# First stage of a fused decoder: four rounds as one program for each of two lanes, a new order of turns, and the extremes found a round later

## The reference

```
x = layernorm(x + L0_attn(x, W_f, b_f, W_i, b_i, W_h, b_h))   # gated linear recurrence along the sequence
x = layernorm(x + L0_xattn(x, ctx, Wq, Wkv, Wout, bout))      # 16 heads of 8, 256 queries, 64 context tokens
# the next block (L0_ffn) first needs max(abs(x)) over the WHOLE x, for its quantisation scale
```

## Time and profile before

| | |
|---|---|
| median of 3 runs | 3333.57 us (3331.22 to 3334.71) |
| the profiled execution | 3336.23 us, span 3334.4 us |
| first stage, from the first R1 on PE to the last norm | 21.9 to 352.2 us |
| busy over the whole span | PE 78%, PEld 56%, DVE 51%, ACT 30%, POOL 11% |
| mean granted TensorE clock | 0.911 of full |

### The profile page before, as it was taken

The page is one execution under the profiler, slowest core; times in us unless marked ns, Lnnn a source line. Parts: engine busy times, 40 slices in busy tenths (PEclk is TensorE's granted clock), DMA queues, the critical chain, the costliest instruction groups (busy, mean ns, idle before and its releaser), DMA issues.

```text
span 3334.4 us, 52950 instructions
## 1 busy us (share of the span) xinstructions
PE 2614.9 (78%) x23038; PEld 1875.8 (56%) x23038; DVE 1698.1 (51%) x4037; ACT 994.8 (30%) x1385; POOL 354.2 (11%) x605
## 2 busy tenths in 40 slices
PE   4666468888889887786687779877798777987778
PEld 3444146767777776654565555655556555565554
DVE  5555735565665654701367541675416654166541
ACT  3333312222322221021232432324323243232432
POOL 0111100110011100063111000110001100010000
PEclk8788658999999998986898999989999899998999
DMA  2000000000000000223600000000000000000000
GB/s 82 1 1 1 2 1 1 8 8 8 1 8 8 8 7 5 91 38 65 171 1 1 1 7 1 1 1 1 7 1 1 1 1 7 0 1 1 1 1 26
DMA packets 39354, 48.14 MB, mean 14 GB/s; under 512 B 7169, under 2 KB 36369, under 8 KB 38354
## 3 DMA queue, kind: packets, MB, share of 16 engines
q1 hardware_dynamic: 33490, 40.43, 4.1%
q0 software_dynamic: 5632, 4.33, 1.0%
HBM read 31.81 MB, written 12.91 MB: 13 GB/s over the span
## 4 chain that ended last, share of the span: by engine, by line
PE 56%; DVE 29%; ACT 6%; issue 4%; POOL 3%; DMA 1%; SPq 0%; DVEq 0%; POOLq 0%; ACTq 0%
PE banks L2396 7%; PE banks L870 6%; DVE wide_area L2272 4%; PE banks L2595 4%; DVE wide_area L1750 2%; PE banks L2385 2%; PE banks L1370 2%; PE banks L2170 2%; PE banks L1335 2%; PE banks L1169 2%; DVE xs L899 2%; DVE weights L2089 1%; PE banks L1403 1%; PE banks L1677 1%; PE banks L2179 1%
## 5 line engine op out<-in xcount | busy, mean ns | idle before, releaser
L2595 PE MATMUL banks<-wA 128*128 128x128 f32 x2664 | 366.9, 291 | 4.2 <-ACT gates L931 2.1
L2595 PEld LDWEIGHTS banks<-wA 128*128 128x128 f32 x2664 | 340.4, 205 | 23.2 <-issue 15.9
L891 DVE BATCH_NORM_STATS2 stats<-banks 128x6 f32<-128x128 f32 x208 | 46.4, 286 | 391.7 <-PE banks L870 363.8
L2272 DVE TENSOR_REDUCE wide_area<-banks 128x8 f32<-128x2048 f32 x64 | 146.8, 2293 | 103.4 <-PE banks L2170 103.4
L906 POOL TENSOR_TENSOR rstd<-moments,eps 128x4 f32<-128x4 f32 x56 | 11.2, 199 | 1431.7 <-DVE moments L895 1431.7
L2253 ACT ACTIVATE weights<-banks 128x2048 f32<-128x2048 f32 x64 | 120.1, 1877 | 96.1 <-PE banks L2179 96.1
L1750 DVE TENSOR_REDUCE wide_area<-banks 128x16 f32<-128x1024 f32 x80 | 94.1, 1218 | 53.2 <-PE banks L1663 53.1
L2396 PE MATMUL banks<-wide_area,big 128*128 128x512 f32 x192 | 85.7, 592 | 0.0
L899 DVE TENSOR_SCALAR xs<-banks,moments,rstd 128x128 f32<-128x128 f32 x208 | 70.9, 404 | 27.0 <-POOL rstd L908 25.5
L2089 DVE TENSOR_TENSOR weights<-banks,wC 128x2048 f32<-128x2048 f32 x32 | 72.2, 2287 | 24.0 <-PE banks L1976 24.0
L891 DVE BATCH_NORM_STATS2 dilvals<-banks 128x6 f32<-128x128 f32 x144 | 32.0, 285 | 96.8 <-PE banks L870 96.8
(11 more groups left out here) (761 smaller groups left out, 6124.8 us busy)
## 6 DMA issues: line engine op xcount, KB each, us to landing
big<-in_wE SPq DMA_DIRECT2D x1, 4096.0 KB, 12.6
weights<-long_kernel SPq DMA_DIRECT2D x8, 512.0 KB, 7.4
conv<-wide_area SPq DMA_DIRECT2D x16, 256.0 KB, 2.5
wC<-in_wC SPq DMA_DIRECT2D x1, 3012.0 KB, 16.7
wC<-in_wG SPq DMA_DIRECT2D x1, 2971.0 KB, 19.2
big<-in_wT SPq DMA_DIRECT2D x1, 2560.0 KB, 11.8
x_all<-in_xT SPq DMA_DIRECT2D x1, 2048.0 KB, 10.4
total<-spread SPq DMA_DIRECT2D x8, 256.0 KB, 2.2
```

The costliest lines, as they stand in the source:

```text
L891: dve.bn_stats(m.stats[:, i, :], self.tokens(i)).then_inc(*sg.up("dve", f"stats{i}"))
L2272: return dve.tensor_reduce(m.peaks[:, k % 2, :, :].rearrange("p t (r c) -> p r t c", r=4)[:, :, :, SPARE[j]], m.bank[:, :, :].rearrange("p ...
L2595: pe.matmul(bank[:, 0:P], m.ident, m.ident, start=True, stop=True)
```

## The change

The four rounds of a lane become one generator for each engine (`start_pe` and so on), and `turns` takes the steps of the two in the order of a string `FIRST` ("n" is lane 0, "f" lane 1), over all rounds at once. The three empty steps of lane 1 are gone. A lane's extremes of round it - 1 are taken in its own next R1, behind its minima, and after the last round only those of round 3 are left. `quant.dve` stands at the end of lane 1's round 0. "first norm" has 5 fillers, not 6.

```
-BUSY = {..., 'first norm': 6, ...}
+BUSY = {..., 'first norm': 5}
+FIRST = "nnffnnfnffnfnfnnfnffnfnfnfnfnfnfnfnfnfnffnnfnffnnnfnnffnfnffnfnfnfnfnfnfnfnfnfnnffnfnnfnfnffnfnnffnfnfnfnfnfnnfnfnffnfnfnfnfnfnfnfnnfnffnfnfnfnfnfnfnfnfnfnfnnfffnnf"
-        extreme = Signals(ctx, nc, "extreme", dve=each(ITERS, "high", "low"))
+        extreme = [Signals(ctx, nc, f"extreme{i}", dve="high low") for i in range(2)]
 first_pool:
-            yield from idle(LaneRecurrent.TICKS + i * LAG)
+            yield from idle(LaneRecurrent.TICKS)
 first_pe, first_act, first_dve:
-            yield from idle(i * LAG)
 first_dve:
-            yield from g.recurrent.dve(dve, it)
+            steps = g.recurrent.dve(dve, it)
+            next(steps)
+            if it:
+                extremes(dve, i, it - 1)
+            yield
+            yield from steps
+        def extremes(dve, i, it):
+            x, at = m.x_all[:, (2 * it + i) * T:(2 * it + i + 1) * T], 2 * it + i
+            dve.wait_ge(*first[i].norm[1].sig.done("act", "out", it))
+            dve.tensor_reduce(highest[:, at:at + 1], x, AX, ALU.max).then_inc(*extreme[i].up("dve", "high"))
+            dve.tensor_reduce(lowest[:, at:at + 1], x, AX, ALU.min).then_inc(*extreme[i].up("dve", "low"))
+        def start_dve(dve, i):
+            for it in range(ITERS // 2):
+                yield from first_dve(dve, i, it)
+                if it == 0 and i == 1:
+                    dve.wait_ge(loaded["wC"], 16)
+                    quant.dve(dve)
 on pool, pe and act, and likewise on dve:
-            for it in range(ITERS // 2):
-                weave(first_pe(pe, 0, it), first_pe(pe, 1, it), first_ticks, 0)
+            turns(start_pe(pe, 0), start_pe(pe, 1), FIRST)
 dve:
-            for it in range(ITERS // 2):
-                weave(first_dve(dve, 0, it), first_dve(dve, 1, it), first_ticks, 0)
-                if it == 0:
-                    dve.wait_ge(loaded["wC"], 16)
-                    quant.dve(dve)
-                else:
-                    extremes(it - 1)
-            extremes(ITERS // 2 - 1)
+            turns(start_dve(dve, 0), start_dve(dve, 1), FIRST)
+            for i in range(2):
+                extremes(dve, i, ITERS // 2 - 1)
```

More of the change, by code:

```diff
@@ L813 @@
 MIDDLE = "nfnfnfnfnfnfnfnfnfnffnfnfnnfnnfnnnffffnfnffnffnn"
-BUSY = {'first1': 2, 'dil_sum0': 7, 'wide scores1': 8, 'lead norm': 10, 'near norm': 1, 'dil_peaks1': 12, 'dil_peaks0': 2, 'lead product': 5, 'wide start': 2, 'gate': 7, 'back0': 3, 'first3': 1, 'first0': 1, 'first norm': 6, 'last norm 0': 9, 'last norm 1': 12, 'last norm 2': 9, 'last norm 3': 12, 'last norm 4': 12, 'last norm 5': 8, 'last norm 7': 1, 'last norm 8': 8, 'retention turned': 7, 'quant whole': 2, 'taken': 20, 'chosen': 5, 'choice start': 8, 'choice same': 4, 'choice bit': 3, 'choice rank': 24}
+BUSY = {'first1': 2, 'dil_sum0': 7, 'wide scores1': 8, 'lead norm': 10, 'near norm': 1, 'dil_peaks1': 12, 'dil_peaks0': 2, 'lead product': 5, 'wide start': 2, 'gate': 7, 'back0': 3, 'first3': 1, 'first0': 1, 'last norm 0': 9, 'last norm 1': 12, 'last norm 2': 9, 'last norm 3': 12, 'last norm 4': 12, 'last norm 5': 8, 'last norm 7': 1, 'last norm 8': 8, 'retention turned': 7, 'quant whole': 2, 'taken': 20, 'chosen': 5, 'choice start': 8, 'choice same': 4, 'choice bit': 3, 'choice rank': 24, 'first norm': 5}
 LAST = "nnfnnfnfnfnfnfnfnfnfnfnfnfnfnffnnnfnffnfnfnfnfnfnfnfnfnfnfnfnnfnfnffnfnfnfnfnfnfnfnfnfnfnfnfnnfnfnffnfnnffnfnfnfnfnfnfnfnfnfnfnfnfnfnfnfnfnfnfnfnfnfnfnfnfnfnfnfnfnfnfnfnfnfnfnfnfnfnfnfnffnfnfnfnffnffnnfnnff"
+FIRST = "nnffnnfnffnfnfnnfnffnfnfnfnfnfnfnfnfnfnffnnfnffnnnfnnffnfnffnfnfnfnfnfnfnfnfnfnfnnffnfnnfnfnffnfnnffnfnfnfnfnfnnfnfnffnfnfnfnfnfnfnfnfnnfnffnfnfnfnfnfnfnfnfnfnfnnfffnnf"
 MIDDLE_ALONE = "nnnnf" * 6
@@ L3243, in _ @@
             long_kernel.act(act)
-            for it in range(ITERS // 2):
-                weave(first_act(act, 0, it), first_act(act, 1, it), first_ticks, 0)
+            turns(start_act(act, 0), start_act(act, 1), FIRST)
             quant.act(act)
@@ L3296, in _ @@
             dve.tensor_scalar(bv2[:, 1:2], col["l1_bv"], 1.75, None, ALU.mult).then_inc(*const.up("dve", "bv_mid"))
-            dve.wait_ge(*extreme.done("dve", f"low{ITERS - 1}", 0))
+            for i in range(2):
+                dve.wait_ge(*extreme[i].done("dve", "low", ITERS // 2 - 1))
             xscale.dve(dve, (highest, lowest))
```

15 lines of the change are left out of this document (11 added, 4 removed).

## The result

The changed kernel took 3314.88 us (median of 10 runs, 3299.81 to 3333.83), the kernel before 3334.54 us (10 runs, 3329.93 to 3344.18): a ratio of 0.995, 95% interval 0.9933 to 0.9967. That is 19.7 us less, where 27 were forecast (3307); it lies in the range given.

The account below looks back on a forecast made before the run. The first stage was taken as bound by chains of waits between engines, no engine full. Order gains of 36.5 plus 0.6 at the end make 37, less 10 for the clock is 27: 3333.6 to 3307 us, range 3296 to 3327.

Parts of the forecast that it names:

- 10 for the clock: First stage: about two falls of PE's clock a round in the new period, 2.5 us lost a round, 10 in all.
- T: Start of the first lane's z in a round, from which the forecast counts its times; 19.62 us after round 2's first matmul.
- X6(0): Lane 0's step ending the first sequence: 29.4 us after T in round 1's order, 28.25 in rounds 0 and 3, 28.9 in 2.
- the walk: The forecast's step-by-step timing of both lanes through norm, two sequences and tail, giving 73.2 us a round against 81.9.
- The 8 us alone: End of a round: lane 1, three steps behind, finishes alone; the forecast said this 8 us would be gone.
- 14.05 us: Second sequence: period from scores to next scores with a lag of one step, 1.8 us worse than 12.2.
- the 6 us: Rounds 0 and 2: loss from the sum if table loads cost the skill page's 2.66 us a switch, with drain.
- amax right after the memset: End of the stage: sign that four fewer reductions would gain 0.6 us, up to the end of POOL's memset.
- (c): Rival for the first stage: PE's clock never falls, the sum stays 37 us, ending at 3296.5; no separate chance given.
- (b): Rival: half clock for most of the period, gain 7 us or less, 3327 to 3340; chance of slower by it 0.08.
- (a): Rival: 0.15 us more for each of ten steps in two periods of four rounds, 12 us lost, near 3319; chance 0.20.
- (d): Rival: lane 0's next round starts no sooner, gain under 5 us, 3330; 0.08 for little or nothing from (b) and (d).

Follow-up runs that it names:

- old_order: The changed kernel with the lanes taking turns exactly as before (three empty steps, lane 1 first); 3334.48 us, ratio 1.0 to the kernel before.
- fill_seven: The changed kernel with six fillers behind lane 0's peaks of the second sequence only (X7); 3302.30 us, ratio 0.9908 to the kernel before.
- lag_three: The changed kernel with lane 0 three steps ahead over all 80 steps, no meeting at a round's end; 3354.55 us, ratio 1.0062 to the kernel before.

## Why the prediction was right, point by point

**The rounds.** This was the core of it, and it held. The sum said 36.5 us from the order less 10 for the clock, 26.5 in the stage; three profiles of the changed kernel show 29.8, 29.6 and 27.2. old_order shows that it is the order. The sum itself can't be followed to the end: with the figures shown, 53.6 behind T in each round, the gains are 8.0, 9.5, 9.7 and 10.3, or 37.6, and nothing shows how 36.5 came out; the X6(0) of 28.25 and 28.9 that the other orders are said to give would have made it larger still. Less the 10 that is 27.6 to 30.4, which fits the measured as well.

**The norm, the seam and the tail.** Statistics at 3.6 behind z, and measured 3.6 to 3.8. q at 9.0 was right for rounds 1 and 2 (8.6 and 8.9) and wrong for 0 and 3 (11.3 and 11.4): the walk has only five fillers and lane 1's z ahead of lane 0's transposes, but there lane 1's N0b stands ahead of q as well. No wait of PE before R1 in rounds 2 and 3, its six records at full clock. From R1 to z, predicted and measured: 21.65 and 21.66, 20.95 and 19.47, 18.6 and 18.35, 18.0 and 17.82. The 8 us alone are gone: in round 1 lane 0's z starts at 167.31 and lane 1's at 169.17, and in rounds 0 and 3 they are as close; in round 2, where lane 0's X9 and X10 go ahead of lane 1's X9, 3.3 us remain. T missed only in round 1, by two terms of opposite sign: I let the full clock of R1 begin with round 2, but it came in round 1 too (2.84 us, where before it was 5.49, timeline of before), and I took the extremes as free everywhere, while in round 1 they cost 1.6.

**The period and the clock.** 14.05 us and 1.3 for a fall, 15.35 in all: measured 15.35, 15.08, 13.95 and 14.66 in rounds 0 to 3. Where no fall is in it, in rounds 0, 1 and 3 of fill_seven, the period is 14.14 to 14.15, so the walk is off by 0.1 us and the fall costs 1.2. It came where I expected it. From z to z of lane 0 I had 44.9 us without falls, by the order of round 1; it was 47.5, 47.3, 46.5 and 45.0. Against that one figure the excess is 2.6, 2.4, 1.6 and 0.1, 6.7 in sum. Against the prediction's own X6(0) for each order (28.25, 29.4, 28.9 and 28.25) it is 3.8, 2.4, 2.1 and 1.2, or 9.5, near the 10 that I had taken. How much of either is the clock and how much the walk is not shown: lane 0's first scores came 13.3, 14.1 and 13.5 us behind z in rounds 0, 2 and 3, not 10.9, since steps of lane 1 stand ahead of them there.

**Table loads.** Four more, as said: 185 records of ScalarE for 181. Predicted 0.9 in round 0 and nothing in round 2, measured 0.9 and 0.5; so VectorE was late in round 2 as well, which the prediction had named as a sign against it. Behind a load the next activation began after 0.02 us (184.34 to 184.36), and the load itself within 0.02 us of the end of the one before it (183.05 to 183.06). The Trainium skill (ScalarE: Activation LUTs, What ACT_TABLE_LOAD costs) states a drain of 1.38 us beside the load; it was on neither side of it here, and neither were the 6 us that the prediction worked out from the page's figure.

**Extremes.** The step "amax was ready at 356.45, the memset ends at 355.88, so 0.6 is won" failed. The wait for amax looked binding because it came last, but the PARTITION_ALL_REDUCE began 5.82 us behind the memset's end after and 5.79 before, whether amax came ahead of that end or behind it; in the twelve other traces, all with amax ahead, it was 5.5 to 5.9. L156 to L287 took 12.80 before and 12.82 after. The term was 0 of 0.6. And the sign given, amax right after the memset, did not come: it was ready 1.8 us ahead of the memset's end, the four reductions (2.4 us) sooner than before.

**The total.** 27 forecast, 19.7 found in the first ten runs, 27 and 29 in the next two sets. What lacked in the first is not in the stage of its profile; it fits the second course of the middle stage, which I had no row for and gave no chance. The total by itself says little: in the profiled execution the stage gave 3.3 us more than the sum and 7.8 were lost behind it. It is the stage that bears the prediction out. The rivals: no fall (c) is out, since every trace shows falls; the half clock through whole periods (b) is out, the stage's clock is 0.82 to 0.84 and in the three profiles no second period was over 15.4 us; looser chains (a) are out for the second sequence, 14.14 where 1.5 us more were supposed; and that the change doesn't do what it says (d) is out by the 343 and 313 us.

## What to carry to other kernels

When two chains share the engines, first find the stretches where one works alone, and change the order of the queues there: that was worth 25 to 28 us of the stage here (341.4 less 316.0 or 313.4), and everything else in the change nothing that could be timed. A longer lag that helps one phase is paid in each phase that it also shifts, so ask of a lag what it puts behind the slowest wait (lag_three's stage was 45 to 47 us longer than the changed kernel's, with R1 behind z). And where the granted clock moves, a few idle matmuls in the one gap ahead of a product that others wait for can keep it up, but look at the next products too, for the fall may only come later. Judge by the stage in several profiles, not by the total.

## What the runs showed of the hardware that I had not expected

- The same instructions in the same order ran in turns of 104.6 to 106.1 us in thirteen traces and, in one, in four turns of 109.2 in a row, with one more fall of the granted clock in a turn: 20.6 us of 3300.
- Six fillers in a gap of 4.65 us (PE busy 2.65 for 1.32) kept the product behind at 1.15 us for 2.09 in all four rounds (clock 1.00 in the gap); in two of them the fall came 5 us behind the start of that product all the same, and the period stayed at 15.3 us.
- PARTITION_ALL_REDUCE began 5.5 to 5.9 us behind the end of the memset ahead of it on POOL in fourteen traces, whether its input was ready 1.8 us before that end or, in before, 0.6 us behind it.
